# A transformer middle on one core: VectorE one quad ahead, ScalarE two ahead, turns in front of the scores

## The chip, the core and the metric

The kernel is one program on one core of a Trainium2 chip. Five engines run side by side, each with its own queue of instructions in a fixed order: TensorE (matrix products into PSUM), VectorE, ScalarE, GpSimd, and SyncE (SP), which starts most of the transfers. They wait for each other by semaphores only. The metric is the device time in microseconds of one execution; lower is better.

## The reference

There are 16 sequences of 128 tokens, 256 features each, 2,048 tokens in all. Four stages follow each other, each added to the running rows `x` with a gate:

```
x = x + tanh(g_xattn[0]) * retention(layernorm(x), ctx, ctx)            # decay scan
x = x + tanh(g_ffn[0])   * moe0(layernorm(x))                           # 8 experts, top 2, capacity, gelu(a)*g
x = x + tanh(g_xattn[1]) * attention(layernorm(x), ctx, ctx, q/k/v)     # padding and causal mask, softmax
x = x + tanh(g_ffn[1])   * moe1(layernorm(x))                           # 8 experts, top 2, silu
```

## The kernel before, in words

The 16 sequences are worked in four quads of four (`NQ = 4`, `QB = 4`); a quad is 512 tokens. The first mixture of experts ends at about 240 us of the profile, the second begins at about 330 us. Between them lies the middle: for each quad the two expert results are fetched and added (combine), the rows are normalised, turned, and go through attention, and the rows after attention are normalised again and routed to the experts of the second mixture.

The order is written out by hand, engine by engine; there is no planner. The steps, for quad `q` or `t`:

- SyncE: `fetch(q)` (L460) loads the expert results of a quad into one of two places; quads 2 and 3 wait until `joined` of quad `q - 2` has released the place (`yk_used`).
- VectorE: `joined(q)` (L1363) is `combine(q)`, six or eight instructions on L1296, and `norm_stats(2, q)` (L1011, L1014). `coefs(n, q)` (L1018) makes the shift of a normalisation once ScalarE has taken the root. `row_terms(q)` (L1338) reads the router's extra column. `highest(q)` (L1345) takes the row maxima of the scores, `shares(q)` (L1354) the reciprocals of the exponents' sums. `mixed_logits(q)` (L1314) builds the router's logits, `attended(q)` (L1326) adds the attention result, `norm_stats(3, q)` and `chosen(q)` (L1360) follow.
- ScalarE: `root(n, q)` (L664), `normalise(n, q)` (L674, L677), `rows_turned(q)` (L823), the copy of the turned rows out of PSUM, `queries_out(q)` (L827, L830), `exponents(q)` (L833, L836), `shares_turned(q)` (L841, L843), and `last_norm(q)` for the normalisation after attention.
- TensorE: `rows_turned(t)`, called "turn" below, 8 transposes of the normalised rows (L1825, L1545), `queries(t)` (L1834, L1551), `router(1, t)` (9 columns for each of 16 matmuls, L1551), `shares_turned(q)` (L1842, L1847), `scores(t)` (a mask matmul L1856 and 16 matmuls L1860), `mixed(q)` (8 columns, L1865, L1872), `attended(q)` (L1875, L1881).
- GpSimd: `share(q)` (L556, L562, L567) does a quarter of the combine of quads 1 to 3; `value_bias(n)` (L514, L519) adds a bias to four blocks of the values of quad 3.

Normalised rows of the middle have one place, `xn[:, 0]`; `PB` takes both the turned rows and the queries; the queries in SBUF have one place. The scores alternate between two banks. Semaphores count, so an order is also a set of numbers: `EV2` numbers the copies out of PSUM in ScalarE's order, and `VAR`, `COEF`, `XN` number the normalisations. In particular a turn waits for the copy of the queries of the quad before it, `mixed(q)` waits for `row_terms(q + 1)`, and the router of quad 2 or 3 waits for `mixed_logits` of two quads back. Ahead of the first turn TensorE runs 32 filler matmuls (L1823).

Of the kernel before, what the change touches and what calls it, by code (L numbers as in the profile page):

```python
# [37 lines left out]
NQ = NB // QB  # L38
# [66 lines left out]
def build(nc, x, ctxt, mask, g_xattn, g_ffn, wg0, w_in, w_out, wq, bq, wk, bk, wvT, wv, bvc, bv, wg1T, w1, w2, cf_d, out):  # L105
    with ExitStack() as ctx:
# [19 lines left out]
        xn = sb("xn", [P, 2, QB, D])  # L126
# [123 lines left out]
        def xn3(q):  # L250

            return 1 - q % 2
# [94 lines left out]
            return PA[:, q % 2, 0:QB * E]  # L347

        EV2 = {}
        for t in range(NQ + 1):  # L350
            for n, q in (("xT2", t), ("qT", t), ("pT", t - 1)):
                if 0 <= q < NQ:
                    EV2[n, q] = len(EV2) + 1

# [2 lines left out]
        for t in range(NQ + 2):  # L357
            for order, norms in ((VAR, ((0, t), (1, t - 1))), (COEF, ((1, t - 2), (0, t))), (XN, ((1, t - 2),))):
                for n, q in norms:
                    if 0 <= q < NQ:  # L360
                        order[n, q] = len(order) + 1
        for t in range(-1, NQ + 2):
            for n, q in ((2, t + 1), (3, t - 2)):
                for order in (VAR, COEF, XN):
                    if 0 <= q < NQ:
                        order[n, q] = len(order) + 1

        def tiles(dram, row0, n):

# [127 lines left out]
        def _(pool):  # L497
# [58 lines left out]
            def share(q):  # L556

                pool.wait_ge(y_in[q], 32)
                n = q * QB + QB - 1
                rows = [yk(q, k)[:, QB - 1, :] for k in range(K)]  # L560
                for k in range(K):
                    ins = pool.tensor_tensor(rows[k], rows[k], gates[:, k * NB + n:k * NB + n + 1]  # L562
                                             .broadcast_to([P, D]), ALU.mult)
                for k in range(K):
                    ins.then_inc(pool_chain, 1)
                    pool.wait_ge(pool_chain, (q - 1) * K + k + 1)
                    ins = pool.tensor_tensor(xs[:, n, :], xs[:, n, :], rows[k], ALU.add)  # L567
                ins.then_inc(share_done, 1)

            pool.wait_ge(gates_ready, 1)  # L570
            share(1)
            for n in range(3 * QB, 4 * QB):
                value_bias(n)
            for q in range(2, NQ):
                share(q)
            pool.drain()

            gate_step = (NQ - 1) * K + 1
# [79 lines left out]
        def _(act):  # L658
# [5 lines left out]
            def root(n, q, scale=1.0):  # L664
                if (n, q) not in ((3, NQ - 2), (3, NQ - 1)):
                    act.wait_ge(var_ready, VAR[n, q])
                m = place(n, q)
                act.activation(lnv[:, m, :], mv[:, m, :, 1], ACT.Ln, bias=c("eps"), scale=scale).then_inc(ln_ready, 1)
                act.wait_ge(ln_ready, VAR[n, q])
                act.activation(rstd[:, m, :], lnv[:, m, :], ACT.Exp, scale=-0.5).then_inc(sd_ready, 1)  # L670
                if n == 2:
                    act.activation(sd[:, m, :], lnv[:, m, :], ACT.Exp, scale=0.5).then_inc(root2_ready, 1)

            def normalise(n, q, dst):  # L674
                act.wait_ge(coef_ready, COEF[n, q])
                for b in range(QB):
                    ins = act.activation(dst[:, b, :], xs[:, q * QB + b, :], ACT.Identity,  # L677
                                         scale=rstd[:, place(n, q), b:b + 1], bias=nmr[:, place(n, q), b:b + 1])
                ins.then_inc(xn_ready if n else xn0_ready, 1)
# [143 lines left out]
            def rows_turned(q):  # L823
                act.wait_ge(evac2_ready, EV2["xT2", q])
                act.activation(xT[:, :, :], PB[:, :, :], ACT.Copy).then_inc(evac2_done, 1)

            def queries_out(q):  # L827
                act.wait_ge(evac2_ready, EV2["qT", q])
                for k in range(DC):
                    ins = act.activation(qT[:, k, :], PB[:, k, :], ACT.Identity, bias=q_bias[:, k:k + 1])  # L830
                ins.then_inc(evac2_done, 1)

            def exponents(q):  # L833
                act.wait_ge(sc_ready, q + 1)
                for b in range(QB):
                    ins = act.activation(prb[:, b, :], scores_at(q)[:, b * S:(b + 1) * S], ACT.Exp,  # L836
                                         bias=att[:, q % 2, 1, b:b + 1], scale=SCALE,
                                         accum_out=att[:, q % 2, 2, b:b + 1])
                ins.then_inc(exp_done, 1)

            def shares_turned(q):  # L841
                act.wait_ge(evac2_ready, EV2["pT", q])
                act.activation(pT[:, :, :], PA[:, 1, :].rearrange("p (b s) -> p b s", b=QB), ACT.Copy)\  # L843
                    .then_inc(evac2_done, 1)

            def last_norm(q):
                if q >= 2:
                    act.wait_ge(xn_out1[xn3(q)], 16)
                normalise(3, q, xn[:, xn3(q)])
# [7 lines left out]
            last_values(NQ - 1)  # L857
            root(2, 0)
            normalise(2, 0, xn[:, 0])
            for t in range(NQ - 1):  # L860
                rows_turned(t)
                if t >= 1:
                    exponents(t - 1)
                root(2, t + 1)
                queries_out(t)
                normalise(2, t + 1, xn[:, 0])
                if t >= 1:
                    shares_turned(t - 1)
            root(3, 0)
            rows_turned(NQ - 1)  # L870
            exponents(NQ - 2)
            last_norm(0)
            queries_out(NQ - 1)
            shares_turned(NQ - 2)
            root(3, 1)
            last_norm(1)
            exponents(NQ - 1)
            shares_turned(NQ - 1)

            def row_sums(q):  # L880
# [118 lines left out]
        def _(dve):  # L999
# [18 lines left out]
            def coefs(n, q):  # L1018

                dve.wait_ge(sd_ready, VAR[n, q])  # L1020
                m = place(n, q)
                link(dve.scalar_tensor_tensor(nmr[:, m, :], mv[:, m, :, 0], -1.0, rstd[:, m, :], ALU.mult, ALU.mult))
                dve.sem_inc(coef_ready, 1)
# [302 lines left out]
            def attended(q):  # L1326

                dve.wait_ge(pv_done, q + 1)
                for b in range(QB):
                    xb = xs[:, q * QB + b, :]  # L1330
                    n = q - NQ + 2
                    ins = dve.scalar_tensor_tensor(xb, PC[:, b // 2, (b % 2) * D:(b % 2 + 1) * D],
                                                   att[:, q % 2, 3, b:b + 1], xb, ALU.mult, ALU.add,
                                                   accum_out=sums[:, n, b:b + 1] if n >= 0 else None)
                link(ins)
                dve.sem_inc(pv_used, 1)

            def row_terms(q):  # L1338

                dve.wait_ge(a_done, q + 1)  # L1340
                link(dve.tensor_scalar(att[:, q % 2, 4, :], logits[:, q * QB:(q + 1) * QB, E], row_term[:, 0:1], None,
                                       ALU.add))
                dve.sem_inc(row_read, 1)
# [16 lines left out]
            def chosen(q):  # L1360
                best_two(lg, range(q * QB, (q + 1) * QB))

            def joined(q):  # L1363
                combine(q)
                dve.sem_inc(yk_used, 1)
                norm_stats(2, q)
# [2 lines left out]
            joined(0)  # L1369
            wide_gates(3)  # L1370
            coefs(2, 0)
            for t in range(NQ - 1):
                joined(t + 1)
                if t >= 2:
                    attended(t - 2)
                coefs(2, t + 1)
                row_terms(t)
                if t >= 2:
                    norm_stats(3, t - 2)
                highest(t)  # L1380
                if t >= 1:
                    shares(t - 1)
                    mixed_logits(t - 1)
                if t >= 2:
                    chosen(t - 2)
            coefs(3, 0)
            attended(NQ - 3)
            norm_stats(3, NQ - 3)
            chosen(NQ - 3)
            row_terms(NQ - 1)  # L1390
            coefs(3, NQ - 3)
            highest(NQ - 1)
            shares(NQ - 2)
            mixed_logits(NQ - 2)
            attended(NQ - 2)
            chosen(NQ - 2)
            dve.sem_inc(chosen_ready, 1)
            shares(NQ - 1)
            mixed_logits(NQ - 1)
# [140 lines left out]
        def _(pe):  # L1540
# [334 lines left out]
            def attended(q):  # L1875
# [6 lines left out]
                                   start=True, stop=True)  # L1882
                mm.then_inc(pv_done, 1)

            for t in range(NQ):
                rows_turned(t)
                if t >= 2:
                    attended(t - 2)
                queries(t)
                router(1, t)  # L1890
                if t >= 1:
                    shares_turned(t - 1)
                scores(t)
                if t >= 1:
                    pe.wait_ge(evac2_done, EV2["pT", t - 1])
                    mixed(t - 1)
            attended(NQ - 2)
            shares_turned(NQ - 1)
            pe.wait_ge(evac2_done, EV2["pT", NQ - 1])
            mixed(NQ - 1)  # L1900
# [112 lines left out]
```

## Time and profile before

| | us |
|---|---|
| median of 3 runs | 573.0 (570.35 to 575.54) |
| the profiled execution | 570.21 |
| its span | 568.3 |
| TensorE busy | 530.6 |
| VectorE busy | 352.2 |
| ScalarE busy | 323.0 |
| GpSimd busy | 257.6 |

Busy times are sums over the whole span. In the trace, PE is TensorE, DVE VectorE, ACT ScalarE, POOL GpSimd; L and a number is the line of the kernel. The release of a wait is named behind an arrow. The matmuls of one step can overlap by a tenth or two of a microsecond, so that the time from one step's start to the next one's is a little less than the row's own duration.

### The profile page before, as it was taken

Reading aid. Unit: us, or ns where it says so; the run is one execution under the profiler, and the core shown is the slowest. Engines: PE = TensorE matmul, PEld = TensorE weight load, DVE = VectorE, ACT = ScalarE, POOL = GpSimd, SP = SyncE. Lnnn points to the kernel's source line nnn. Section 1 sums busy time; section 2 is a strip of 40 time slices with the busy share of each in tenths; the row PEclk is TensorE's granted clock in tenths of the full one; section 3 lists DMA queues with packets and bytes.
Section 4 is the critical chain, followed back from the end, with each engine's and each line's share of the span. In section 5 each row is a group of like instructions: output and inputs, shape, how many; then the busy total and the mean of one; then the engine's idle time right before and its main releaser. Section 6 shows DMA issues by size and latency. Waiting matters only on the chain.

```text
span 568.3 us, 11990 instructions
## 1 busy us (share of the span) xinstructions
PE 530.6 (93%) x3775; PEld 492.4 (87%) x3776; DVE 352.2 (62%) x836; ACT 323.0 (57%) x673; POOL 257.6 (45%) x288
## 2 busy tenths in 40 slices
PE   2899989999999999998997899999999999999993
PEld 0689879999999999986786889999999999999993
DVE  2887855755655665656677866475636574655742
ACT  3572535665656665545577647565646574754742
POOL 2400366664365543325000354556656466654554
PEclk9995899999999999999998799999999999999998
DMA  7954253445345353362033344644544545262233
GB/s 253 383 177 149 66 162 115 153 149 175 92 148 175 97 180 120 111 226 82 0 112 125 81 134 96 194 116 113 120 118 98 142 111 124 46 195 42 40 51 46
DMA packets 52453, 72.74 MB, mean 128 GB/s; under 512 B 7200, under 2 KB 43936, under 8 KB 52416
## 3 DMA queue, kind: packets, MB, share of 16 engines
q1 hardware_dynamic: 40752, 50.34, 27.0%
q0 software_dynamic: 11664, 21.94, 17.3%
q8 instruction: 19, 0.31, 0.2%
q14 instruction: 18, 0.15, 0.1%
HBM read 51.54 MB, written 20.73 MB: 127 GB/s over the span
## 4 chain that ended last, share of the span: by engine, by line
PE 85%; DVE 8%; ACT 2%; issue 2%; DMA 1%; POOL 1%; another core or an unknown queue 0%; SPq 0%; DVEq 0%
PE PA L1727 29%; PE PC L1727 9%; PE PD L1727 9%; PE PC L1941 6%; PE PD L1941 6%; PE PC L1943 3%; PE PD L1943 3%; PE PB L1551 2%; PE PC L1576 2%; PE PC L1551 2%; PE PB L1916 2%; PE PA L1551 2%; PE PB L1739 2%; PE PD L1551 2%; PE PB L1545 1%
## 5 line engine op out<-in xcount | busy, mean ns | idle before, releaser
L1727 PE MATMUL PA<-xhi,w_parts 128*128 128x256 f32 (+1 forms) x880 | 182.7, 289 | 5.1 <-issue 3.2
L1727 PEld LDWEIGHTS PA<-xhi,w_parts 128*128 128x128 f32 x880 | 144.8, 190 | 9.4 <-issue 5.8
L1727 PE MATMUL PA<-xlo,w_parts 128*128 128x256 f32 (+1 forms) x440 | 125.8, 286 | 0.0
L1282 DVE TENSOR_TENSOR hlo<-cT_all,hhi 128x512 fp32r<-128x512 f32 x78 | 54.1, 694 | 95.5 <-ACT hhi L958 92.5
L956 ACT ACTIVATE cT_all<-PA 128x512 f32<-128x512 f32 x78 | 46.8, 600 | 89.8 <-PE PA L1727 89.1
L622 POOL DMA_INDIRECT out<-ys,row_o x38 | 65.0, 1709 | 70.3 <-DVE ys L1491 64.5
L1727 PEld LDWEIGHTS PA<-xlo,w_parts 128*128 128x128 f32 x440 | 83.6, 190 | 0.0
L528 POOL DMA_INDIRECT xg<-xn_rows,row_x x45 | 46.1, 1024 | 67.8 <-DVEq L1137 41.5
L537 POOL DMA_INDIRECT y_rows<-ys,row_y x40 | 41.9, 1048 | 54.7 <-ACT ys L776 51.3
L1941 PE MATMUL PC<-w_parts,hhi 128*128 128x512 f32 x160 | 58.4, 398 | 0.0
L598 POOL DMA_INDIRECT xg<-xn_rows,row_x x44 | 48.0, 1092 | 22.7 <-POOL slot_gate L616 8.7
L1727 PE MATMUL PC<-xhi,w_parts 128*128 128x256 f32 (+1 forms) x256 | 55.6, 295 | 0.2 <-DVE ring L1248 0.2
L1941 PE MATMUL PD<-w_parts,hhi 128*128 128x512 f32 x144 | 52.5, 398 | 0.0
L1727 PE MATMUL PD<-w_parts,hhi 128*128 128x256 f32 x280 | 51.7, 285 | 0.4 <-issue 0.4
L958 ACT ACTIVATE hhi<-cT_all 128x512 fp32r<-128x512 f32 x78 | 49.4, 633 | 2.5
L1943 PE MATMUL PC<-w_parts,hlo 128*128 128x256 f32 x160 | 45.0, 281 | 0.0
L1727 PEld LDWEIGHTS PD<-w_parts,hhi 128*128 128x128 f32 x280 | 43.6, 191 | 0.6 <-issue 0.6
L1727 PEld LDWEIGHTS PC<-xhi,w_parts 128*128 128x128 f32 x256 | 42.9, 190 | 0.8 <-DVE ring L1248 0.4
L1282 DVE TENSOR_TENSOR w_parts<-raw,w_parts 128x512 fp32r<-128x512 f32 x64 | 40.8, 688 | 3.2 <-ACT w_parts L812 3.0
L1943 PE MATMUL PD<-w_parts,hlo 128*128 128x256 f32 x144 | 40.5, 281 | 0.0
L1727 PE MATMUL PD<-w_parts,hlo 128*128 128x256 f32 x140 | 39.6, 283 | 0.0
L1727 PE MATMUL PC<-xlo,w_parts 128*128 128x256 f32 (+1 forms) x128 | 37.5, 293 | 0.0
(273 smaller groups left out, 1074.3 us busy)
## 6 DMA issues: line engine op xcount, KB each, us to landing
raw<-w SPq DMA_DIRECT2D x16, 1024.0 KB
raw<-L_ffn_W_in SPq DMA_DIRECT2D x8, 1024.0 KB
raw<-L_ffn_W_out SPq DMA_DIRECT2D x8, 512.0 KB
y_rows<-ys SPq DMA_DIRECT2D x8, 512.0 KB, 8.1
xn_rows<-xn SPq DMA_DIRECT2D x8, 512.0 KB, 3.5
xs<-x SPq DMA_DIRECT2D x4, 512.0 KB, 6.3
cx<-ctx SPq DMA_DIRECT2D x4, 512.0 KB, 7.0
ys<-y_rows SPq DMA_DIRECT2D x4, 512.0 KB, 4.2
```

The source lines that it names most:

```text
L528: pool.indirect_dma_start(xg[:, s, :], None, xn_rows[0].ap(), bass.IndirectOffsetOnAxis(ap=row_x[:, e % E * CT + t:e % E * CT + t + 1], ax ...
L537: pool.indirect_dma_start(y_rows.ap(), bass.IndirectOffsetOnAxis(ap=row_y[:, e * CT + t:e * CT + t + 1], axis=0), ys[:, s, :], None).then_ ...
L598: pool.indirect_dma_start(xg1[j % SLOTS1], None, xn_rows[1].ap(), bass.IndirectOffsetOnAxis(ap=row_x[:, j:j + 1], axis=0)).then_inc(g1_in[ ...
L622: pool.indirect_dma_start(out, bass.IndirectOffsetOnAxis(ap=row_o[:, j:j + 1], axis=0), ys[:, j % SLOTS1, :], None, compute_op=ALU.add).th ...
L956: act.activation(group1(h1, g), PA[:, g % 2, :], ACT.Silu).then_inc(silu_done, 1)
L958: act.activation(group1(hhi, g), group1(h1, g), ACT.Copy).then_inc(h1_hi, 1)
L1282: return dve.tensor_tensor(dst, src, hi.bitcast(F32), ALU.subtract)
L1551: mm = pe.matmul(dst, a, b, start=(k == 0), stop=(k == len(lhs) - 1))
L1576: pe.matmul(at[:, 0, 0:P], ident, decay, start=True, stop=True)
L1727: mm = pe.matmul(dst, a[k], b[k], start=(first and k == 0 and a is lhs_hi and b is rhs_hi), stop=(last and k == n - 1 and a is lhs_lo))
L1941: pe.matmul(y1_at(par, t), hhi[:, a:a + P], w_parts[:, :, at], start=(g == 0 and n == 0), stop=False)
L1943: mm = pe.matmul(y1_at(par, t)[:, 0:D], hlo[:, a:a + P], whi[:, at], start=False, stop=(g == GROUPS - 1 and n == 1))
```

## The change

Only orders change; no instruction is added or removed. On GpSimd, `share(2)` goes ahead of the value biases. On VectorE, `joined(2)` goes ahead of `row_terms(0)`, and `joined(3)` behind `shares(0)`; `attended`, `norm_stats(3, ...)` and `shares` of a quad go one step earlier. On ScalarE, `normalise(2, t + 2)` stands in step `t`, ahead of `exponents(t)`. On TensorE, the turn of quad `t + 1` goes ahead of `scores(t)`, and `attended(t - 1)` right behind `mixed(t - 1)`.

```
-        for t in range(NQ + 1):
-            for n, q in (("xT2", t), ("qT", t), ("pT", t - 1)):
+        for t in range(-1, NQ + 1):
+            for n, q in (("qT", t), ("xT2", t + 1), ("pT", t - 1)):
                 if 0 <= q < NQ:
                     EV2[n, q] = len(EV2) + 1
...
-        for t in range(-1, NQ + 2):
-            for n, q in ((2, t + 1), (3, t - 2)):
+        for n in (2, 3):
+            for q in range(NQ):
                 for order in (VAR, COEF, XN):
-                    if 0 <= q < NQ:
-                        order[n, q] = len(order) + 1
+                    order[n, q] = len(order) + 1
...
             pool.wait_ge(gates_ready, 1)
             share(1)
+            share(2)
             for n in range(3 * QB, 4 * QB):
                 value_bias(n)
-            for q in range(2, NQ):
-                share(q)
+            share(3)
             pool.drain()
...
             normalise(2, 0, xn[:, 0])
-            for t in range(NQ - 1):
-                rows_turned(t)
+            rows_turned(0)
+            root(2, 1)
+            queries_out(0)
+            normalise(2, 1, xn[:, 0])
+            for t in range(NQ):
                 if t >= 1:
-                    exponents(t - 1)
-                root(2, t + 1)
-                queries_out(t)
-                normalise(2, t + 1, xn[:, 0])
+                    queries_out(t)
+                if t + 1 < NQ:
+                    rows_turned(t + 1)
                 if t >= 1:
                     shares_turned(t - 1)
-            root(3, 0)
-            rows_turned(NQ - 1)
-            exponents(NQ - 2)
-            last_norm(0)
-            queries_out(NQ - 1)
-            shares_turned(NQ - 2)
-            root(3, 1)
-            last_norm(1)
-            exponents(NQ - 1)
+                if t + 2 < NQ:
+                    root(2, t + 2)
+                    normalise(2, t + 2, xn[:, 0])
+                else:
+                    root(3, t + 2 - NQ)
+                    last_norm(t + 2 - NQ)
+                exponents(t)
             shares_turned(NQ - 1)
...
             coefs(2, 0)
-            for t in range(NQ - 1):
-                joined(t + 1)
-                if t >= 2:
-                    attended(t - 2)
-                coefs(2, t + 1)
-                row_terms(t)
-                if t >= 2:
-                    norm_stats(3, t - 2)
-                highest(t)
-                if t >= 1:
-                    shares(t - 1)
-                    mixed_logits(t - 1)
-                if t >= 2:
-                    chosen(t - 2)
+            joined(1)
+            coefs(2, 1)
+            joined(2)
+            row_terms(0)
+            highest(0)
+            coefs(2, 2)
+            shares(0)
+            joined(3)
+            row_terms(1)
+            highest(1)
+            coefs(2, 3)
+            mixed_logits(0)
+            attended(0)
+            norm_stats(3, 0)
+            shares(1)
+            chosen(0)
+            row_terms(2)
             coefs(3, 0)
-            attended(NQ - 3)
-            norm_stats(3, NQ - 3)
-            chosen(NQ - 3)
-            row_terms(NQ - 1)
-            coefs(3, NQ - 3)
-            highest(NQ - 1)
-            shares(NQ - 2)
-            mixed_logits(NQ - 2)
-            attended(NQ - 2)
-            chosen(NQ - 2)
+            highest(2)
+            mixed_logits(1)
+            attended(1)
+            norm_stats(3, 1)
+            shares(2)
+            chosen(1)
+            row_terms(3)
+            coefs(3, 1)
+            highest(3)
+            mixed_logits(2)
+            attended(2)
+            chosen(2)
             dve.sem_inc(chosen_ready, 1)
...
+            rows_turned(0)
             for t in range(NQ):
-                rows_turned(t)
-                if t >= 2:
-                    attended(t - 2)
                 queries(t)
                 router(1, t)
+                if t + 1 < NQ:
+                    rows_turned(t + 1)
                 if t >= 1:
                     shares_turned(t - 1)
                 scores(t)
                 if t >= 1:
                     pe.wait_ge(evac2_done, EV2["pT", t - 1])
                     mixed(t - 1)
-            attended(NQ - 2)
+                    attended(t - 1)
             shares_turned(NQ - 1)
```

## Rows read from the trace of the kernel before

**Rows 1.** The page's first line.

```profile
span 568.3 us, 11990 instructions
```

**Rows 2.** Busy times by window: us, PE, PEld, DVE, ACT, POOL busy (instructions), clock, DMA, GB/s.

```profile
264.00:320.00 56.00, 50.30 (x312) 40.40 (x312) 42.70 (x174) 39.64 (x117) 5.12 (x9) 0.94 0.23 74
```

**Rows 3.** The chain of waits in the middle: start, us, what.

```profile
285.56 2.08 ACT xn L677 x4
```

**Rows 4.** Timeline of TensorE: start, us, engine, line, operation, out<-in, count, idle before.

```profile
262.25 1.85 PE L1551 MATMUL PD<-wg,xT 128*128 128x9 f32 x16
...
264.17 1.95 PE L1860 MATMUL PA<-cT_all,cx 128*128 128x128 f32 x16
265.95 1.04 PE L1545 MATMUL PB<-cf,xn 128*128 128x128 f32 x8
268.10 3.70 PE L1551 MATMUL PB<-xT,wqkv 128*128 128x512 f32 x8 [1.11 <-ACT xT L825]
...
273.34 0.63 PE L1847 MATMUL PA<-cf,xg 128*128 128x128 f32 x4
...
276.62 1.06 PE L1872 MATMUL PD<-vg,xg 128*128 128x8 f32 x8 [0.39 <-ACT xg L843]
...
278.44 1.89 PE L1881 MATMUL PC<-vv,xg 128*128 128x256 f32 x8
...
291.73 3.60 PE L1551 MATMUL PB<-xT,wqkv 128*128 128x512 f32 x8
...
304.61 3.66 PE L1881 MATMUL PC<-vv,xg 128*128 128x256 f32 x8
```

**Rows 5.** Timeline of ScalarE in the middle.

```profile
261.64 0.30 ACT L668 ACTIVATE lnv<-mv,cf 128x4 f32<-128x4 f32 x1 [2.98 <-DVEq L1016]
...
262.45 1.27 ACT L830 ACTIVATE cx<-PB,q_bias 128x512 f32<-128x512 f32 x2 [0.18 <-PE PB L1551]
263.60 2.07 ACT L677 ACTIVATE xn<-xs,nmr,rstd 128x256 f32<-128x256 f32 x4
...
267.94 0.36 ACT L836 ACTIVATE xg<-PA,att 128x128 f32<-128x128 f32 x1
...
269.22 0.22 ACT L836 ACTIVATION_READ_ACCUMULATOR xg<-PA,att 128x1 f32 x1
...
283.44 0.30 ACT L668 ACTIVATE lnv<-mv,cf 128x4 f32<-128x4 f32 x1 [2.38 <-DVEq L1016]
```

**Rows 6.** Timeline of VectorE in the middle.

```profile
254.40 2.67 DVE L1296 SCALAR_TENSOR_TENSOR xs<-xg,gates,xs 128x256 f32<-128x256 f32 x3
...
262.21 0.16 DVE L1022 SCALAR_TENSOR_TENSOR nmr<-mv,rstd 128x4 f32<-128x4 f32 x1 [0.66 <-ACT rstd L670]
...
266.15 0.69 DVE L1349 TENSOR_REDUCE att<-PA 128x4 f32<-128x512 f32 x1 [1.79 <-PE PA L1860]
...
267.44 2.82 DVE L1296 SCALAR_TENSOR_TENSOR xs<-ys,gates,xs 128x256 f32<-128x256 f32 x6 [0.16 <-DVE att L1351]
...
278.77 1.28 DVE L1296 SCALAR_TENSOR_TENSOR xs<-xg,gates,xs 128x256 f32<-128x256 f32 x3
```

**Rows 7.** Timeline of GpSimd in the middle.

```profile
255.00 3.52 POOL L519 TENSOR_TENSOR vv<-vv,bvb 128x256 f32<-128x256 f32 x4
...
265.07 0.61 POOL L562 TENSOR_TENSOR xg<-xg,gates 128x256 f32<-128x256 f32 x1 [3.43 <-DMA ring<-y_rows]
```

**Rows 8.** Timeline of the queue of SyncE in the middle.

```profile
251.47 0.91 SPq L462 DMA_DIRECT2D ys<-y_rows  x2
259.67 0.36 SPq L462 DMA_DIRECT2D xg<-y_rows  x1
```

**Rows 9.** Timeline of TensorE ahead of the first mixture of experts.

```profile
43.03 1.85 PE L1551 MATMUL PC<-wg,xT 128*128 128x8 f32 x16
```

**Rows 10.** Busy times by window, columns as in Rows 2.

```profile
44.00:46.00 2.00, 2.00 (x17) 2.00 (x17) 1.54 (x15) 0.80 (x4) 0.00 (x0) 0.81 0.30 99
...
304.00:305.00 1.00, 1.00 (x8) 1.00 (x8) 0.87 (x12) 0.93 (x4) 0.00 (x0) 0.82 0.02 8
```

## The prediction, made before the changed kernel ran

> **What bounds the kernel now.** I read the page's first line, then the busy times by stage, then the chain of waits, then the timelines of the engines one by one through the middle. The middle runs from 256.6 us, when TensorE turns the first quad's normalised rows, to about 322 us; only here is anything moved. Its share is small: the span is 568.3 us [rows 1], so 1% of the kernel is 5.7 us, about the smallest change that a measurement of this kernel can tell from none. The stage from 264 to 320 us has TensorE busy 50.3 of 56 us, VectorE 42.7, ScalarE 39.6, GpSimd 5.1 [rows 2]. So TensorE has little idle time to give back, and neither of the other two is full. The chain of waits agrees: it goes through TensorE, with one excursion over VectorE that ends in the normalisation of quad 3 at 285.56 us [rows 3]. The question is therefore where TensorE idles, and which queue it waits for.
>
> Quad 0 is typical [rows 4]: queries, then the router at 262.25, the scores from 263.95 (the mask first, 0.22 us, then 1.78 us of matmuls from 264.17), quad 1's turn at 265.95, then a gap of 1.1 us until ScalarE has copied the turned rows, and quad 1's queries at 268.10. The next gaps are smaller: 0.39 us ahead of mixed(0) at 276.62 by the row, 0.6 with its weight load. From 262.25 to 291.73, where quad 3's queries start, are 29.5 us; by the prices below the work in them is 26.9, and 2.5 are idle.
>
> **The work of each step, from the rows.** On TensorE I go from one step's start to the next one's, which is the row's duration less an overlap of 0.15 [rows 4]: turn 0.9, queries 3.45, router 1.7 (with the mask, 262.25 to 264.17), shares turned 0.47, mask and scores 2.0, mixed 0.92, attended 1.73. Three routers, scores and turns, two of each other step: 5.1 + 6.0 + 2.7 + 6.9 + 0.9 + 1.8 + 3.5 = 26.9. ScalarE [rows 5]: queries out 1.27, normalise 2.07, exponents 1.50 (267.94 to the end of the last of their eight instructions, 269.22 + 0.22). VectorE [rows 6]: joined, from its first combine at 278.77 to the root that it releases at 283.44 [rows 5], 4.67; root to coefs 0.57 (261.64 to 262.21); highest, from 266.15 to the next instruction at 267.44, 1.29. TensorE's count of instructions is unchanged, and so is everybody else's: every edit is a move. So the cost is only in waits.
>
> **The start.** The first normalisation, turn and queries stand where they stood. GpSimd now has share(2) ahead of four value biases (3.52 us for four, [rows 7]). A fetch lands 5.4 us after its issue: the one issued at 259.67 [rows 8] releases GpSimd at 265.07 [rows 7], so the fetch of quad 2, issued from 251.47 on [rows 8], lands near 256.9. GpSimd idles for some 1.8 us that it filled before, and combine(1) on VectorE goes faster there: three combines take 2.67 us beside GpSimd and 1.28 us alone [rows 6]. That is a gain of up to 1.9 us for quad 1's statistics, and it is worth nothing: ScalarE runs queries_out(0) at 262.45 ahead of normalise(2,1) in both orders, and starts that at 263.60 [rows 5]. The value biases end near 263.5, against a first use at attended(0) near 280: no cost. combine(2) now runs at the contended price, 6 x 0.89 = 5.3 us from about 260.5, so its root stands ready near 268.4; what needs it comes at 270.1 (below). That is the cover, 1.7 us. SP's fetches follow the combines and come earlier. The copy of the queries and the turns change their counts on a semaphore and cost nothing.
>
> **Turn(1) ahead of scores(0).** Its rows are ready at 263.60 + 2.07 = 265.67. Before, scores(0) filled TensorE until then. Now TensorE stands behind turn(1)'s wait from 263.95 to 265.75: **a new gap of 1.8 us**. Behind it are queued turn(1), 0.9, and scores(0), 2.0, which end at 268.65 instead of 265.95. The gap ahead of queries(1) goes: they start at 268.65 instead of 268.10, +0.55 only.
>
> **The long chain from scores(0).** highest(0) starts 0.2 later, 268.85; on VectorE coefs(2,2) is queued behind it: 270.14. ScalarE starts normalise(2,2) 0.25 later (as at 262.21 and 262.45), 270.40 to 272.47, and only behind it the exponents of quad 0, which end at 273.87 instead of 269.44. Two things wait for them. First, queries_out(1) is queued behind the exponents: 273.87 + 1.27 = 275.05 or so. TensorE has queries(1) and router(1) done at 268.65 + 3.55 + 1.7 = 273.9 and waits with turn(2) until 275.1: **a second gap of 1.2 us**. Turn, shares turned and scores(1) then run to 275.1 + 0.9 + 0.47 + 2.0 = 278.45. Second, shares(0) on VectorE waits for the exponents, and joined(3) is queued behind it: 273.87 + 0.5 + 4.67 = 279.1. row_terms(1) stands behind joined(3), an instruction of the size of coefs (0.16 us, [rows 6]) with its release 0.3. mixed(0) needs it and starts at 279.4: **a third gap of 0.95 us**. Then 0.92 + 1.73 put queries(2) at 282.05, where they stood near 280.17 (278.44 + 1.73).
>
> **Quads 2 and 3.** highest(1) to 280.7, coefs(2,3), normalise(2,3) to 283.0 and exponents(1) to 284.4 are all early enough: queries(2) and router(2) last to 287.2, turn(3) needs queries_out(2), done at 286.9, and finds its rows ready. Turn 0.9, shares 0.47, scores 2.0, mixed 0.92, attended 1.73 follow without a gap: queries(3) at 293.2 to 293.3 instead of 291.73 [rows 4]. On VectorE highest(2) comes at 290.8, just behind coefs(3,0) at 290.4, whose root ScalarE has queued behind the copy of shares(1). From queries(3) on, the order of TensorE is what it was, shares(2) is out of VectorE's tail (0.5 us, in a time when attended(2) waited for TensorE anyway), and the tail moves along. Sum without the clock: gaps 1.8 + 1.2 + 0.95 against 2.5 lost ones: **+1.5 us**, the same as 293.25 - 291.73.
>
> **The clock.** No row shows a gap of this kind in this place, so its cost is bounded. TensorE ran at its full 2.4 GHz through the middle, and fell towards 1.2 GHz between 304 and 305 (mean 0.82, [rows 10]), just behind it; attended(3) then took 3.66 us against 1.89 of the same work [rows 4], +1.8. At 44 to 46 us it fell too, while TensorE was busy 2.00 of 2.00 us, with matmuls of 8 columns from 43.03 on [rows 9, 10]. After the change the router's 9-column matmuls (1.7 us) and the 1.8 us gap stand side by side, 262.25 to 265.75: 3.5 us with nothing wide in them. In the middle of before I find no such stretch over 2.0 us that kept the clock. Ends: 0 and 3 x 1.8 = 5.4 us, one fall for each new gap. I take one fall, +1.8, by the row at 304.61 that it is nearest to; it lands on turn(1) and scores(0), the head of the long chain, so it counts in full. The Trainium skill ("TensorE: Matmul & The Clock Gate", section "HAM oscillation") ties the fall to idle gaps between bursts of matmuls; by it alone the router's matmuls would count as work, a gap not much longer than the 1.1 us that kept the clock would most likely leave it, and the sum would be +1.5 us. The busy stretch at 44 to 46 us speaks against that reading.
>
> **Forecast.** +1.5 + 1.8 = +3.3 us. The profiled execution took 570.21 us (its span and 1.9 around it), 2.8 us below the median of three, 573.0; the middle of the four executions shown is 571.7. I go from there: 571.7 + 3.3 = 575.0 us; from the profile's own time it would be 573.5.
>
> **Rivals.** (a) *No fall of the clock*: +1.5, 573.2 us. For it: gaps of 1.1 us did no harm before. Against: the 3.5 us stretch. (b) *Faster*: the place is the wait of queries(1) and the waits of mixed. If ScalarE and VectorE turn round faster than by my rows, so that the rows of turn(1) and row_terms(1) are there when TensorE comes, the old gaps are gone and no new ones come: -2.5 + small rest, 571.7 - 1.9 = 569.8 us. It decides where the two new waits together (1.8 + 0.95) and the copy behind the exponents (1.2) fall below 2.5 us; the rows put them at 3.95. Against it: normalise(2,1) starts behind queries_out(0) in both orders, so the 1.8 cannot shrink by VectorE's early finish. (c) *Several falls*: the gaps at 275 and 279 stand beside router(1) and mixed(0), narrow too. 1.5 + 5.4 = +6.9, 578.6 us. (d) The change's ahead-work is real, as each queue is a fixed order; there is no case in which it does nothing.
>
> **Chances.** Forecast 0.50, (a) 0.25, (b) 0.12, (c) 0.13. The range reaches from near (b), 570.5, to (c), 578.6. More than 1% faster needs over 5.7 us, more than TensorE's idle: 0.03, for the spread of the runs (570.35 to 575.54). More than 1% slower: (c) and a little, 0.16. Within 1%: 0.81.
>
> **What would show it.** Right: TensorE idle about 1.8 us ahead of turn(1); scores(0) ending near 268.6 or, with the clock at 0.5, near 270; the exponents of quad 0 behind a normalise; turn(2) waiting for the copy of the queries; mixed(0) waiting for row_terms(1); quad 3's queries 1.5 us later, 3.3 with one fall. Wrong: no gap ahead of turn(1), queries(2) at 280 or sooner, or queries(3) before 291.7.

## The result and the profile after

The changed kernel takes 574.85 us in the median of 20 runs (571.03 to 578.65) against 572.92 us of the kernel before (567.84 to 575.54, 20 runs). The ratio is 1.0049 with a 95% interval of 1.0029 to 1.0068: slower by 1.7 to 3.9 us, and within 1%. So a change of half a percent can be told from none here, where the prediction took 1% for the smallest such change. The profiled execution took 575.25 us with a span of 573.3, 5.0 more than before.

TensorE's timeline of the changed kernel, to be held against [rows 4] (columns as there):

```profile
257.47 1.09 PE L1549 MATMUL PB<-cf,xn 128*128 128x128 f32 x8 [1.69 <-ACT xn L676]
259.68 5.29 PE L1555 MATMUL PB<-xT,wqkv 128*128 128x512 f32 x8 [1.11 <-ACT xT L824]
264.81 1.85 PE L1555 MATMUL PD<-wg,xT 128*128 128x9 f32 x16
268.29 1.09 PE L1549 MATMUL PB<-cf,xn 128*128 128x128 f32 x8 [1.63 <-ACT xn L676]
269.43 1.95 PE L1864 MATMUL PA<-cT_all,cx 128*128 128x128 f32 x16
271.22 3.60 PE L1555 MATMUL PB<-xT,wqkv 128*128 128x512 f32 x8
...
277.65 1.07 PE L1549 MATMUL PB<-cf,xn 128*128 128x128 f32 x8 [1.15 <-ACT cx L829]
...
282.02 1.03 PE L1876 MATMUL PD<-vg,xg 128*128 128x8 f32 x8 [0.87 <-DVEq L1342]
282.91 1.97 PE L1885 MATMUL PC<-vv,xg 128*128 128x256 f32 x8
...
295.82 3.60 PE L1555 MATMUL PB<-xT,wqkv 128*128 128x512 f32 x8
```

The three new gaps are there, each with the releaser that the prediction named: 1.63 us ahead of turn(1) for the normalised rows, 1.15 ahead of turn(2) for the copy of the queries, 0.87 ahead of mixed(0) for row_terms(1). The gap ahead of queries(1) is gone. The three gaps together are 3.65 us. From router(0) to queries(3) are 295.82 - 264.81 = 31.0 us, against 291.73 - 262.25 = 29.5 before [rows 4].

The chain of waits now runs through the long chain that the prediction laid out. The same stretch in it (start, us, what):

```profile
271.42 0.70 DVE att L1348
...
272.64 0.17 DVE nmr L1021
...
272.90 2.07 ACT xn L676 x4
274.98 1.39 ACT xg L835 x8
276.36 0.02 issue
276.39 0.19 DVE att L1356
...
276.86 1.29 DVE xs L1295 x3
278.17 1.29 DVE xs L1295 x3
...
279.63 1.42 DVE stats L1010 x4
...
281.60 0.23 DVE att L1340
...
282.02 1.03 PE PD L1876 x8
```

Read it downwards: maxima of the scores, coefs(2,2) behind them, normalise(2,2), the exponents of quad 0, shares(0), joined(3), row_terms(1), mixed(0). Before, the chain was on TensorE up to 276.24 us and only then on VectorE, through highest(1) and joined(3), to the normalisation of quad 3 [rows 3]; the chain before, where it changes over:

```profile
274.19 2.06 PE PD L1860 x16
276.24 0.02 issue
276.27 0.70 DVE att L1349
```

The other 3.5 us of the longer span are not gaps of the new order. The first turn starts 0.9 us later, as the first fetch landed later (VectorE waited 2.11 us for it, and 0.26 before). Queries(0) take 5.13 us from start to start instead of 3.54, because the clock fell there. The windows of the changed kernel (columns as in [rows 2]):

```profile
258.00:260.00 2.00, 0.89 (x7) 0.65 (x5) 1.79 (x8) 1.02 (x1) 1.85 (x3) 0.88 0.35 64
260.00:262.00 2.00, 2.00 (x3) 0.85 (x3) 1.21 (x3) 0.60 (x3) 2.00 (x3) 0.50 1.02 343
262.00:264.00 2.00, 2.00 (x5) 0.76 (x4) 1.97 (x3) 0.00 (x0) 2.00 (x4) 0.77 0.35 121
264.00:266.00 2.00, 2.00 (x15) 1.52 (x13) 1.82 (x4) 0.99 (x2) 1.92 (x4) 1.00 0.00 0
...
264.00:300.00 36.00, 32.20 (x195) 25.30 (x196) 22.10 (x87) 22.06 (x60) 3.03 (x5) 1.00 0.12 43
```

This fall stands ahead of router(0), and so ahead of every new gap. Through the three new gaps, from 264 to 300 us, this execution kept the clock at 1.00.

The last 1.4 us lie in the second mixture of experts: 239.7 us from its first matmul to the end against 238.3, while the stretch from queries(3) to that matmul is 0.5 shorter.

### The profile page after: what moved, and what is told of

The parts are those of the page before. It is cut to its first block, busy times and chain, and to the rows that moved or that the text cites. A ratio compares the mean times of both kernels' runs of the same rounds, so it can differ in the third digit from the quotient of the medians.

```text
span 573.3 us, 11988 instructions
## 1 busy us (share of the span) xinstructions
PE 529.2 (92%) x3771; PEld 491.6 (86%) x3776; DVE 350.4 (61%) x836; ACT 322.9 (56%) x673; POOL 258.5 (45%) x288
## 4 chain that ended last, share of the span: by engine, by line
PE 74%; DVE 7%; issue 6%; DMA 5%; ACT 4%; POOL 2%; DVEq 0%; SPq 0%; POOLq 0%; ACTq 0%
PE PA L1731 26%; PE PD L1731 8%; PE PC L1731 7%; PE PC L1945 6%; PE PD L1945 6%; PE PC L1947 3%; PE PD L1947 3%; PE PB L1555 2%; PE PB L1920 2%; DMA xg<-xn_rows,row_x 2%; DVE stats L1010 1%; ACT xn L676 1%; PE PC L1555 1%; PE PB L1743 1%; PE PA L1555 1%
```

## The experiments

Three theories. **Order**: the three gaps cost 1.5 us and nothing else counts (B in the expectations). **Order and clock**: beside them the clock falls in some executions, where a gap and narrow matmuls stand together (A). **Any instruction** in the gap keeps the clock (C). Each kernel below was timed in 12 executions; a ratio is to the kernel before in the same session, with its 95% interval. The profiled executions differ by up to 9 us in where the first turn stands (252.5 to 261.6), ahead of anything that the edits touch, so I read the order from the time between router(0) and queries(3), and the clock from the windows.

**Fillers in the new gaps.** In the changed kernel, on TensorE:

```
             for t in range(NQ):
                 queries(t)
                 router(1, t)
+                if t < 2:
+                    busy((6, 4)[t])
                 if t + 1 < NQ:
                     rows_turned(t + 1)
...
                     pe.wait_ge(evac2_done, EV2["pT", t - 1])
+                    if t == 1:
+                        busy(3)
                     mixed(t - 1)
```

> The changed order, with filler matmuls (128 columns, results unused) in its three new gaps on TensorE: six ahead of turn(1), four ahead of turn(2), three ahead of mixed(0). Theory A (part of the loss is the clock, which falls beside the gaps in some executions): 1 to 2 us faster than the changed kernel, ratio to before about 1.002, and the clock at 1.0 from 264 to 300 us in the profile. Rival B (the clock keeps through the gaps anyway; the loss is the three waits and nothing else): the same as the changed kernel or a few tenths slower, ratio 1.005.

Ratio 0.9999 (0.9971 to 1.0027), 568.83 us, against 1.0050 for the unedited changed kernel beside it (the first repeat below): 2.9 us faster, more than the 1 to 2 expected. TensorE's timeline of this kernel shows the order as slow as without the fillers, within 0.1 us, 291.47 - 260.52 = 30.95 us:

```profile
260.52 1.85 PE L1555 MATMUL PD<-wg,xT 128*128 128x9 f32 x16
262.23 1.58 PE L1580 MATMUL PC<-cf 128*128 128x128 f32 x12
264.00 1.09 PE L1549 MATMUL PB<-cf,xn 128*128 128x128 f32 x8 [0.19 <-ACT xn L676]
...
291.47 3.60 PE L1555 MATMUL PB<-xT,wqkv 128*128 128x512 f32 x8
```

Six fillers are x12 in the rows. The clock stays up; its windows:

```profile
258.00:264.00 6.00, 5.81 (x36) 4.19 (x34) 4.95 (x15) 3.82 (x9) 4.76 (x7) 1.00 0.50 166
264.00:280.00 16.00, 15.73 (x107) 13.24 (x108) 9.14 (x36) 9.06 (x25) 1.10 (x2) 1.00 0.00 1
280.00:300.00 20.00, 20.00 (x126) 15.84 (x125) 12.84 (x64) 12.90 (x37) 0.00 (x0) 1.00 0.23 80
```

The waits are all still there, only filled, and the loss is gone. So B alone is out: gaps of this length do not cost the timed loss by themselves. The profiles do not say where all of the 2.9 us went: from router(0) to queries(3) this one is only 0.3 us shorter than that of the first repeat.

**scores(0) ahead of turn(1) again.**

```
                 router(1, t)
+                if t == 0:
+                    scores(0)
                 if t + 1 < NQ:
                     rows_turned(t + 1)
                 if t >= 1:
                     shares_turned(t - 1)
-                scores(t)
+                if t >= 1:
+                    scores(t)
```

> The changed order, but scores(0) ahead of turn(1) on TensorE, as before the change; all else as changed. My chain of waits: the gap ahead of turn(1) (1.8 us) goes, and quad 0's exponents end 1.6 us earlier; with them turn(2), joined(3) and mixed(0) come 1.6 us earlier. Expected 1.5 us faster than the changed kernel, which is the time of the kernel before within a few tenths: ratio to before 1.000 to 1.002. Rival: if only the clock cost time, or the loss lies elsewhere (VectorE's or ScalarE's order), it stays at 1.005.

Ratio 0.9996 (0.9969 to 1.0024), as expected. The profiled execution has 30.62 us from router(0) to queries(3), with a fall of the clock in scores(1) in it (3.14 us from start to start where it takes 1.79). Most of that is covered: row_terms(1) on VectorE starts at 276.05, which by the distance in the changed kernel (281.60 to 282.02) lets mixed(0) start at 276.47, and it started at 277.08. So my estimate is a cost of 0.6 us and 30.0 us without the fall, a third of the way from the order before (29.5) to the changed one (31.0). The timing shows that this one exchange heads the long chain; the profile shows that a part of the order's cost, the wait for row_terms(1), stays.

**Exponents ahead of normalise(2,2).**

```
+                if t == 0:
+                    exponents(t)
                 if t + 2 < NQ:
                     root(2, t + 2)
                     normalise(2, t + 2, xn[:, 0])
...
-                exponents(t)
+                if t >= 1:
+                    exponents(t)
```

> The changed order, but on ScalarE exponents(0) ahead of root(2,2) and normalise(2,2). My chain: shares(0) and joined(3) start 2 us sooner, so mixed(0) no longer waits for row_terms(1) (0.95 us gained), while turn(2) waits as long as before (for the copy of the queries, now behind normalise(2,2)). Expected 0.9 us faster than the changed kernel, ratio to before 1.003 to 1.004; the profile shows no gap ahead of mixed(0) and still about 1.2 us ahead of turn(2). Rival: the wait for row_terms(1) is covered by another one that ends as late: no gain.

Ratio 1.0050 (1.0022 to 1.0079): no gain, a miss. The gap ahead of mixed(0) went, but turn(2) now waits 1.67 us instead of 1.15: the root of quad 2, which ran while ScalarE waited for the maxima, now stands between the exponents and the copy of the queries (268.73 to 269.37 in this profile). And the clock fell on turn(1) and scores(0) (4.26 us for both against 2.93). Without that fall the 31.75 us from router(0) to queries(3) would be 30.4, 0.6 less than in the changed kernel; the timing does not resolve that.

**The changed kernel again, twice.**

> The changed kernel once more, unedited, for a second profile on the same chip. Order alone (A and B): router(0) to queries(3) takes 31.0 us again. The fall of the clock at quad 0's queries and the late first fetch, seen in the first profile of the changed kernel, belong to the execution and not to the order: they need not come again, and the span is then 1.5 to 2.5 us shorter than 573.3. If they belong to the change they come again.

> The changed kernel, unedited, once more beside these: ratio to before 1.003 to 1.007, and a fall of the clock between 257 and 278 us in the profile, as in its first two profiles. If the clock holds in this one, the falls are a matter of chance and not of every execution.

Ratios 1.0050 (1.0026 to 1.0075) and 1.0075 (1.0047 to 1.0103). The two profiles differ in where the clock falls. In the first it falls on turn(2), at 274.7, and costs 0.24 us only, since scores(1) had slack before mixed(0): 31.25 us from router(0) to queries(3). In the second it falls on scores(0), as predicted, and once more on turn(2). TensorE's timeline, first the row of turn(2) in the first repeat and then the second repeat, with its windows:

```profile
274.70 1.94 PE L1549 MATMUL PB<-cf,xn 128*128 128x128 f32 x8 [1.16 <-ACT cx L829]
```

```profile
267.09 1.85 PE L1555 MATMUL PD<-wg,xT 128*128 128x9 f32 x16
270.56 1.09 PE L1549 MATMUL PB<-cf,xn 128*128 128x128 f32 x8 [1.63 <-ACT xn L676]
271.71 3.58 PE L1864 MATMUL PA<-cT_all,cx 128*128 128x128 f32 x16
275.12 3.60 PE L1555 MATMUL PB<-xT,wqkv 128*128 128x512 f32 x8
...
281.55 1.59 PE L1549 MATMUL PB<-cf,xn 128*128 128x128 f32 x8 [1.15 <-ACT cx L829]
...
300.27 3.60 PE L1555 MATMUL PB<-xT,wqkv 128*128 128x512 f32 x8
```

```profile
270.00:272.00 2.00, 1.39 (x10) 1.40 (x12) 1.82 (x5) 0.82 (x3) 1.13 (x2) 0.93 0.00 0
272.00:274.00 2.00, 2.00 (x11) 2.00 (x11) 0.81 (x6) 1.31 (x4) 0.00 (x0) 0.50 0.00 0
274.00:276.00 2.00, 2.00 (x10) 1.52 (x9) 0.68 (x1) 0.00 (x0) 0.00 (x0) 0.72 0.03 8
```

From router(0) to queries(3) are 33.2 us: 31.0 of the order, 1.6 for the fall on scores(0) (3.41 against 1.79 from start to start), 0.55 for the second. The fall at queries(0) of the first profile did not come again in these two, but it did in the next run, though TensorE's order is the same as before up to there. It is no mark of the new gaps.

**Narrow fillers.** As the first experiment, but with 8 columns each:

```
+            def narrow(count):
+                for n in range(count):
+                    pe.matmul(PC[:, 0, 0:E], ident, decay[:, 0:E], start=True, stop=True)
...
+                if t < 2:
+                    narrow((6, 4)[t])
```

> As e1_fill, with the same thirteen filler matmuls in the same places, but each of 8 columns instead of 128: TensorE has instructions in the gaps, of the same length as the router's. Theory A (narrow matmuls do not keep the clock): the profile shows a fall to 0.5 between 260 and 280 us, as in the changed kernel, and the ratio to before is near 1.005. Rival C (any instruction in the gap keeps the clock): as e1_fill, no fall, ratio 1.000. Rival B (no clock in it at all): as the changed kernel, but then e1_fill's gain stays unexplained.

Ratio 1.0028 (0.9998 to 1.0059), which lies between and tells the theories apart badly. Beside the unedited changed kernel of its session (1.0075) it is 0.0047 lower, with an error of 0.004, about as much as the wide fillers gave in theirs (0.0051): the timing does not show that wide fillers help more than narrow ones. Only the profile tells them apart. TensorE's timeline:

```profile
258.62 5.40 PE L1555 MATMUL PB<-xT,wqkv 128*128 128x512 f32 x8 [1.11 <-ACT xT L824]
263.86 1.85 PE L1555 MATMUL PD<-wg,xT 128*128 128x9 f32 x16
265.56 1.48 PE L1891 MATMUL PC<-cf 128*128 128x8 f32 x12
...
275.40 1.15 PE L1891 MATMUL PC<-cf 128*128 128x8 f32 x8
276.69 1.94 PE L1549 MATMUL PB<-cf,xn 128*128 128x128 f32 x8
278.43 1.06 PE L1851 MATMUL PA<-cf,xg 128*128 128x128 f32 x4
```

```profile
274.00:276.00 2.00, 2.00 (x20) 2.00 (x19) 0.50 (x3) 2.00 (x11) 0.00 (x0) 1.00 0.00 0
276.00:278.00 2.00, 1.85 (x11) 1.79 (x11) 1.97 (x5) 0.55 (x1) 0.00 (x0) 0.55 0.00 0
```

TensorE has no gap over 0.2 us from 273.70 to 279.6, and turn(2) still runs at half speed (1.74 us from start to start, granted clock 0.50 from 277 to 278). The fall comes behind the router and the fillers, and costs 1.0 us up to mixed(0) (5.34 us from turn(2) against 4.37 in the changed kernel). So C, as it is put, is out. The same profile has a fall at queries(0), ahead of any filler: 5.24 us from start to start.

**The kernel before with fillers**, four behind turn(0) and four behind turn(1), and the kernel before unedited:

```
                 rows_turned(t)
+                if t < 2:
+                    busy(4)
```

> The kernel before with wide fillers in its own two gaps of 1.1 us (four behind turn(0), four behind turn(1)); router(0) to queries(3) stays at 29.5 us. If the kernel before also loses to a fall of the clock in some executions, it gains: ratio 0.997 to 0.999. If its gaps are harmless (as in its profile): 1.000.

> The kernel before with wide fillers in its two gaps of 1.1 us, repeated: ratio 0.997 again if the kernel before loses to falls of the clock in part of its executions; 1.000 if f3's gain was the spread of the runs.

> The kernel before, unedited: ratio 1.000 (what the measurement makes of no change), and a second profile of it. If falls of the clock belong to the changed order alone, none between 255 and 300 us; if they come in both, one may stand here too.

Filled: 0.9972 (0.9941 to 1.0003) and 1.0008 (0.9977 to 1.0039); unedited: 1.0015 (0.9991 to 1.0038). The gain of the first did not come again; if there is one, the runs do not show it. Both profiles of the kernel before hold the clock from 256 to 300 us, and so do both filled ones. From router(0) to queries(3) the second has 29.6 us. Its window:

```profile
256.00:300.00 44.00, 40.26 (x243) 31.05 (x246) 30.22 (x117) 26.65 (x72) 6.82 (x10) 1.00 0.18 61
```

**The changed kernel with all gaps filled**, the four fillers behind turn(0) added to the first experiment (one more line, `busy(4)`, behind `rows_turned(0)`):

> The changed order with wide fillers in its three new gaps, as e1_fill, and four more in the old gap behind turn(0). No fall of the clock between 255 and 300 us; router(0) to queries(3) 31.0 us. Against g2_before_fill (29.5 us, clock kept too) this is the price of the order alone: +1.5 us, ratio 1.0027 to g2. If the loss of the changed kernel were the clock alone, the two would be the same; if it were the order alone, they would stand 0.005 apart.

Ratio 0.9995 (0.9962 to 1.0027), 30.95 us from router(0) to queries(3), clock 1.00 from 256 to 300 us. In the profiles the order costs 1.3 to 1.5 us against the filled kernel before (29.45 and 29.70); in the timing the changed order is 0.0013 lower, with an error of 0.0045, so the predicted 0.0027 is neither shown nor excluded.

**A better version**: the changed kernel with scores(0) ahead of turn(1), row_terms(1) ahead of joined(3), and wide fillers in what is left:

```
             rows_turned(0)
+            busy(4)
             for t in range(NQ):
                 queries(t)
                 router(1, t)
+                if t == 0:
+                    scores(0)
+                if t == 1:
+                    busy(2)
                 if t + 1 < NQ:
                     rows_turned(t + 1)
+                if t == 0:
+                    busy(4)
                 if t >= 1:
                     shares_turned(t - 1)
-                scores(t)
-                if t >= 1:
+                    scores(t)
...
             shares(0)
+            row_terms(1)
             joined(3)
-            row_terms(1)
```

> The changed order with scores(0) ahead of turn(1), row_terms(1) ahead of joined(3) on VectorE, and wide fillers in what gaps are left (four behind turn(0), four behind turn(1), two ahead of turn(2)). By my chain of waits queries(3) comes 28.5 to 28.7 us after router(0) against 29.5 before and 31.0 in the changed kernel; with the clock kept: ratio to before 0.996 to 0.998. Rival (the middle is not where the time is): the 28.6 us come and the ratio stays at 1.000 or above.

> The version of f2_best repeated: router(0) to queries(3) 29.0 us as there, 0.5 less than before, no fall of the clock in that stretch. Ratio 0.996 to 0.998 to the kernel before and 0.001 below g2_before_fill.

Ratios 0.9974 (0.9943 to 1.0005) and 0.9982 (0.9949 to 1.0015), 29.0 and 28.7 us from router(0) to queries(3) (28.5 to 28.7 expected of the first), clock 1.00 from 256 to 309 us. Weighted by their intervals the two give 0.9978 (0.9955 to 1.0000): about 1.3 us faster than the kernel before, at the edge of what can be told, and clearly faster than the changed kernel. From the kernel before with fillers (0.9990, 0.9968 to 1.0012, pooled in the same way) it cannot be told.

## Why the prediction was right

The time came out at 574.85 us where 575.0 was forecast. The order's part of the mechanism is borne out step by step. That the sum hit so closely is in part luck: the base was 571.7 us where the kernel before measured 572.92, and the clock's part came out in another place and size in each profile.

*The start* held. share(2) was released at 257.94, 5.6 us after its fetch; combine(1) ran uncontended (1.28 and 1.28 us, against 2.67 for three in [rows 6]); combine(2) took 4.84 us where 5.3 was said. As predicted, all of it stayed without effect: ScalarE had quad 1's root at 260.08 and then waited 4.30 us for the queries.

*The three gaps* were 1.63, 1.15 and 0.87 us for 1.8, 1.2 and 0.95, and the sum of the order 31.01 - 29.48 = 1.53 us for 1.5. Where the gaps were filled with wide matmuls it was 1.47 (30.95 in both). The claim that the chain starts with scores(0) behind turn(1) is shown: undoing that exchange alone took the timed loss away (0.9996 against 1.0050 beside it). That the copy of the queries holds turn(2) is shown by its releaser. It is not the exponents alone that hold the copy: with them ahead of normalise(2,2) the copy still came behind both, 0.5 us later after highest(0) than in the changed kernel.

*The clock.* A fall stands between 256 and 300 us in every profile of the changed order without wide fillers, six of six, and in none of the four with them, nor in the four of the kernel before, filled or not. But only in five of the six does one stand beside a new gap, and only once in three profiles of the unedited changed kernel on the step that the prediction named:

| profile | step on which the clock fell | cost, us |
|---|---|---|
| changed kernel, first | queries(0), ahead of every new gap | 1.6 |
| changed kernel, first repeat | turn(2) | 0.24 |
| changed kernel, second repeat | scores(0); turn(2) | 1.6; 0.55 |
| scores(0) ahead of turn(1) | scores(1) | 0.6 |
| exponents first | turn(1) and scores(0) | 1.3 |
| narrow fillers | queries(0); turn(2) | 1.7; 1.0 |

So a fall that costs 1.8 us on turn(1) and scores(0), the prediction's term, was right as a kind of event and as its price there (1.6), and wrong as the event of every execution. The row that the price came from cost its own kernel less than 1.8: from queries(3) to the first matmul of the second mixture are 38.3 us in the profile with that fall, and 38.0 in the second profile of the kernel before, where attended(3) took 1.97 us.

*The sum does not close.* Pooled over the sessions, weighted by their intervals, the changed kernel stands at 1.0055 (1.0042 to 1.0069) and with wide fillers at 0.9997 (0.9976 to 1.0019): 3.3 us, with an error of 1.4, come back with the fillers. The falls of its three profiles cost 1.6, 0.24 and 2.2 us, 1.3 in the mean. That these falls are what the fillers give back is therefore argued, not shown; the narrow fillers, with two falls in their profile, gained nearly as much in the timing. And the order's +1.5 us, which is in every profile, is not visible in the timing. It would be a ratio of 1.0026, just outside the interval of the filled changed kernel against the kernel before. Against the filled kernel before (0.9990) it is within the error.

*Open.* In two of the three profiles of the changed kernel the second mixture of experts is 1.4 to 1.7 us longer than before, with one wait for gathered rows; in the timeline of TensorE of the first repeat it is this row:

```profile
341.69 0.80 PE L1920 MATMUL PB<-cf,xg 128*128 128x128 f32 x4 [1.47 <-DMA xg<-xn_rows,row_x]
```

The version with scores(0) ahead of turn(1) waits 1.16 us in the same place, and its timed ratio is 0.9996 all the same. The kernel before, its filled form, the filled changed kernels, the narrow fillers and the second repeat show no wait over 0.2 us there. Whether the order brings it, or the execution, was not tried. It may be part of the 3.3 us.

*The rule of the Trainium skill* ("TensorE: Matmul & The Clock Gate", section "HAM oscillation") was weighed as tying the fall to idle gaps between bursts. The trace of the narrow fillers does not agree with that reading: they left no gap over 0.3 us ahead of turn(1) or turn(2), and the clock fell on turn(2) all the same. The measurement decides.

*The rivals.* (a), no fall, is out: its 573.2 us were +1.5, a ratio of 1.0026, and the pooled interval starts at 1.0042. (b), faster, would have needed gaps below 2.5 us together; they were 3.65. (c), several falls, is what the second repeat's execution shows (two of them, 578.36 us), but the median stayed below it. The 0.25 given to (a) was much: a fall stood in each of the three profiles, and its place and price were what varied.

## What to carry to other kernels

Moving a producer (here the turn) in front of ready work (here the scores) pays only if its own input is there by then; otherwise the ready work, and every queue behind its result, waits with it. One such exchange headed the whole loss here. Before such a move, look at the granted clock beside the gaps too: one fall cost between 0.24 and 1.7 us here, by the step that it met, and the gaps' own cost was 1.5. One profile is not enough to place such a fall; three of the same kernel put it in three places. Dummy matmuls of full width in a gap that cannot be closed are cheap (2.9 us came back here) and a good test. Put both versions through it before blaming an order, and add up whether what comes back is what the profile had shown as lost.

## What the runs showed of the hardware

The granted clock of TensorE fell from 1.0 to 0.5, which are 2.4 and 1.2 GHz, eight times between 256 and 300 us in the six profiles of the table. Five of the falls came behind the router's 9-column matmuls and 0.7 to 1.6 us of idle. One came behind 9-column and 8-column matmuls with no idle over 0.2 us (narrow fillers, 276 us). Two came at queries(0), behind a turn with idle on both sides of it (1.69 and 1.11 us in the first profile, 0.64 and 1.11 with the narrow fillers). Neither brings a fall each time: the first profile passed the router and gaps of 1.63, 1.15 and 0.87 us at 1.00, and the second repeat passed idle of 1.27 and 1.11 us around the first turn. With thirteen 128-column fillers in the new gaps the clock kept 1.00 in two profiles of two, and in the two of the better version with its ten. From router(0) to queries(3) the changed kernel lost 0, 0.24 and 2.2 us to falls in its three profiles.

VectorE's combine instructions took 0.43 us each while GpSimd was idle and 0.81 us each, 4.84 for six, while it ran the value biases and share(3), in the same profile of the changed kernel.
